# One block for each attention's layer norm and projections, by chunks of four tiles, with its elementwise work spread over three engines

## What is computed

```python
x = x + _L0_attn_ref(_layernorm(x), Wq, Wk, Wv, Wo)            # first attention, no biases
x = x + _L1_attn_ref(_layernorm(x), Wq, bq, Wk, bk, Wv, bv, ...)   # second, biased; its result is
                                                               # added to the normalised x
_layernorm(x) = (x - mean(x)) / sqrt(var(x) + eps)
q, k, v = xn @ Wq.T (+ bq), xn @ Wk.T (+ bk), xn @ Wv.T (+ bv)
```

## Time and profile before

| | us |
|---|---|
| median of three runs (2930.15 to 2933.18) | 2932.02 |
| the profiled execution | 2926.32 |
| its span, first to last instruction | 2924.5 |
| n2 and p2, from 176.3 to 250.3 of the span | 74.0 |
| n5 and p5, from 1109.5 to 1178.4 | 68.9 |

### The profile page before, as it was taken

One profiled execution on the slowest core, in us unless ns is written; L12 is line 12 of the kernel. 1 busy time (PEld: TensorE's weight loads), 2 busy tenths in 40 slices (PEclk: granted clock), 3 DMA queues, 4 the chain that ended last, 5 costly groups with the idle time before them and its releaser, 6 DMA issues. The chain is left out here.

```text
span 2924.5 us, 60113 instructions
## 1 busy us (share of the span) xinstructions
PE 2454.6 (84%) x18614; PEld 1007.0 (34%) x18614; DVE 2460.5 (84%) x3972; ACT 2229.3 (76%) x2441; POOL 1969.5 (67%) x1247
## 2 busy tenths in 40 slices
PE   2756999998586995799999999999999999983898
PEld 2642333333484663122222222222222222222566
DVE  4667888885577666899999999999999999996765
ACT  4433777777364553599999999999999999993554
POOL 4520222222463662599999999999999999994465
PEclk9966999999596997699999999999999999997799
DMA  3223100000121002100000000000000000000000
GB/s 116 70 59 98 30 28 29 28 28 12 42 60 29 1 0 71 38 16 17 15 14 14 16 16 14 14 15 16 14 14 15 16 14 14 15 5 0 1 12 18
DMA packets 93505, 76.58 MB, mean 26 GB/s; under 512 B 32481, under 2 KB 73961, under 8 KB 93265
## 3 DMA queue, kind: packets, MB, share of 16 engines
q1 hardware_dynamic: 89104, 66.36, 7.9%
q0 software_dynamic: 4288, 8.82, 0.9%
HBM read 47.77 MB, written 24.42 MB: 25 GB/s over the span
## 5 line engine op out<-in xcount | busy, mean ns | idle before, releaser
L1800 POOL TENSOR_TENSOR a_sg<-a_sg,all_f0w 128x1568 f32<-128x1568 f32 x256 | 904.9, 3535 | 21.4
L1943 ACT ACTIVATE a_pt<-a_pb 128x1024 f32<-128x1024 f32 x512 | 708.4, 1384 | 10.3 <-PE a_pb L1850 10.3
L2029 DVE TENSOR_SCALAR a_sg<-a_pa 128x1024 int32<-128x1024 int32 x512 | 615.5, 1202 | 8.0 <-PE a_pa L1850 7.9
L2018 DVE TENSOR_REDUCE a_mx<-a_pm 128x1 f32<-128x1024 f32 x507 | 613.7, 1210 | 8.8 <-PE a_pm L1850 7.3
L1952 ACT ACTIVATE a_sg<-a_sg,a_parh 128x2048 f32<-128x2048 f32 x256 | 605.1, 2364 | 15.3 <-POOL a_sg L1800 15.3
L1868 PE MATMUL a_po<-a_pt,a_Vh 128*32 128x512 f32 x2048 | 538.4, 604 | 65.0 <-ACT a_osb L1962 62.7
L1956 ACT ACTIVATE a_sg<-a_sg 128x2048 f32<-128x2048 f32 x256 | 584.1, 2282 | 0.1
L1868 PE MATMUL a_po<-a_sg,a_Vh 128*32 128x512 f32 x2048 | 538.3, 604 | 0.0
L1797 POOL TENSOR_SCALAR all_f0w<-a_sg,a_parh 128x1568 f32<-128x1568 f32 x256 | 513.9, 2007 | 27.8 <-DVE a_sg L2029 25.0
L1610 ACT ACTIVATE a_pt<-a_ring 128x1024 f32<-128x1024 f32 (+2 forms) x384 | 313.7, 846 | 150.8 <-PE a_ring L1537 147.5
L1682 DVE TENSOR_REDUCE a_mx<-a_ring 128x2 f32<-128x1024 f32 (+3 forms) x384 | 359.0, 955 | 71.6 <-PE a_ring L1520 52.6
(11 more groups left out here) (268 smaller groups left out, 4535.6 us busy)
## 6 DMA issues: line engine op xcount, KB each, us to landing
all_Q<-q_parts SPq DMA_DIRECT2D x256, 48.0 KB
all_K<-k_parts SPq DMA_DIRECT2D x256, 48.0 KB
k_parts<-p_parts SPq DMA_DIRECT2D x16, 384.0 KB, 3.1
e_recs<-routed_rows SPq DMA_DIRECT2D x70, 64.5 KB, 1.9
n_xn<-expert_rows SPq DMA_DIRECT2D x16, 256.0 KB, 4.4
all_Q<-a_rows SPq DMA_DIRECT2D x256, 2.0 KB
q_parts<-p_parts SPq DMA_DIRECT2D x16, 192.0 KB, 2.4
q_parts<-p_parts SPq DMA_DIRECT2D x8, 384.0 KB, 2.6
```

The costliest lines, as they stand in the source:

```text
L1800: nc.gpsimd.tensor_tensor(buf[:, :, 0:CUT], buf[:, :, 0:CUT], sums, ALU.mult)\
L1943: nc.scalar.activation(pt[(j - LT) % 4][:, i, :], pb[:], ACT.Exp, scale=SC)\
L2018: nc.vector.tensor_reduce(mx[:, (j // PER) % 2, t:t + 1], top[:], AX.X, ALU.max)\
L2029: nc.vector.tensor_scalar(sg[(j - ls) % 4][:, i, :].bitcast(I32), pa[:].bitcast(I32), SIGN_OFF, None, ALU.bitwise_and).then_inc(abs_done, 1)
```

## The change

The two blocks become one, `norm_project`, which goes by chunks of four tiles in 11 steps. In step k, VectorE finishes the scale of chunk k and takes the statistics of chunk k+1; ScalarE normalises chunk k (no longer VectorE), copies the transposes of chunk k-1 and splits the two pieces of chunk k-2; TensorE projects chunk k-2 and transposes chunk k-1; VectorE makes the remainders and copies the values of chunk k-2. GpSimd makes the low parts (no longer VectorE) and, in the second attention, the residual addition, one instruction for four tiles in place of four. `xn` becomes a ring of three chunks, and the transposes' PSUM ring two banks in place of four. The four chained instructions of the scale become three and a fourth that makes the bias of the normalisation. The result of the feed-forward is loaded into `XNT` in place of `xn`. The first stacks' transfers go behind pieces 6 to 11, two each, in place of three each behind pieces 8 to 11.

```diff
--- before.py
+++ after.py
...
-def ln_transposed(nc, tag, X, XNT, ident, add_to_x=False, split=None, router=None, incoming=None):
+def ln_transposed(nc, tag, X, XNT, ident, split=None, router=None, incoming=None):
...
-                def add(k):
-                    pool.wait_ge(xn_ready, k + 1)
-                    nc.gpsimd.tensor_tensor(X[:, k, :], X[:, k, :], xn[:, k, :], ALU.add).then_inc(x_added, 1)
...
-                if add_to_x:
-                    for k in range(NT):
-                        add(k)
...
-def project(nc, tag, XNT, V, qd, kd, w, weights_in, biased, ones, paired=False, constants=None, stack_loads=(),
-            cleared=None, sharpness=None):
+def norm_project(nc, tag, X, XNT, V, qd, kd, ident, w, weights_in, biased, ones, cleared, stack_loads, paired=False,
+                 incoming=None, constants=None, sharpness=None, add_to_x=False):
...
+    XR = 3
...
+        xn = m.sb("xn", [P, XR, 4, D])
         parts = m.sb("parts", [P, 4, SPLIT, CH], BF16)
         rest = m.sb("rest", [P, 4, CH])
...
+        pt = m.ps("pt", [P, 2, CH])
         psq = m.ps("psq", [P, 4, CH])
         psv = m.ps("psv", [P, 2, 4, D])
...
-        early = {i: stack_loads[n:n + 3] for n, i in zip(range(0, len(stack_loads), 3), range(8, 12))}
-
+        EARLY = 6
+        early = {i: stack_loads[n:n + 2] for n, i in zip(range(0, len(stack_loads), 2), range(EARLY, 2 * NCH))}
         pieces = range(2 * NCH)
+        steps = range(-1, NCH + 2)
...
+                if incoming is not None:
+                    for c in range(NCH):
+                        sp.dma_start(XNT[:, c * CH:(c + 1) * CH].rearrange("p (k d) -> p k d", d=D),
+                                     incoming[c * CH:(c + 1) * CH, :].rearrange("(k p) d -> p k d", p=P))\
+                            .then_inc(came[c], 16)
...
-                    if i == 8:
+                    if i == EARLY:
...
+                def low(i):
+                    pool.wait_ge(mid_done, i + 1)
+                    nc.gpsimd.tensor_tensor(parts[:, i % 4, 2, :], rest[:, i % 4, :], parts[:, i % 4, 1, :],
+                                            ALU.subtract).then_inc(lo_done, 1)
+
+                def add(c):
+                    pool.wait_ge(xn_ready, 4 * c + 4)
+                    nc.gpsimd.tensor_tensor(X[:, tiles(c), :], X[:, tiles(c), :], xn[:, c % XR], ALU.add)\
+                        .then_inc(x_added, 1)
+
+                for k in steps:
+                    if add_to_x and 0 <= k < NCH:
+                        add(k)
+                    if 0 <= k - 2:
+                        low(2 * (k - 2))
+                        low(2 * (k - 2) + 1)
+
+                def project(c, n):
+                    i = 2 * c + n
+                    if n == 0:
+                        pe.wait_ge(evacuated, c + 1)
+                    if i >= 4:
+                        pe.wait_ge(rest_done, i - 3)
+                    tokens, out = XNT[:, c * CH:(c + 1) * CH], psq[:, i % 4, :]
+                    if paired and n == 0:
+                        tokens = tokens.rearrange("p (c g n) -> p g c n", g=2, n=P)
+                        out = out.rearrange("p (g c n) -> p g c n", g=2, n=P)
+                    nc.tensor.matmul(out, (wqT, wkT)[n][:], tokens, start=True, stop=True).then_inc(q_done, 1)
+
+                def turn(c):
+                    pe.wait_ge(xn_ready, 4 * c + 4)
+                    if c >= 2:
+                        pe.wait_ge(evacuated, c - 1)
+                    for q in range(4):
+                        last = nc.tensor.transpose(pt[:, c % 2, q * P:(q + 1) * P], xn[:, c % XR, q, :], ident[:])
+                    last.then_inc(turned, 1)
+
...
+                pe.wait_ge(weights_in, loads)
+                for k in steps:
+                    if 0 <= k - 2:
+                        project(k - 2, 0)
+                        project(k - 2, 1)
+                    if 0 <= k - 1 < NCH:
+                        turn(k - 1)
+                    if 0 <= k - 2:
+                        values(k - 2)
+
+                nc.scalar.preload_act_table_set("natural_log_exp_and_others")
...
+                def root(c):
+                    act.wait_ge(ve_ready, c + 1)
+                    nc.scalar.activation(rs[:, tiles(c)], ve[:, tiles(c)], ACT.Ln).then_inc(ln_var, 1)
+                    act.wait_ge(ln_var, c + 1)
+                    nc.scalar.activation(rs[:, tiles(c)], rs[:, tiles(c)], ACT.Exp, scale=-0.5).then_inc(rs_ready, 1)
+
+                def normalise(c):
+                    act.wait_ge(scaled, c + 1)
+                    if c >= XR:
+                        act.wait_ge(turned, c - XR + 1)
+                        if add_to_x:
+                            act.wait_ge(x_added, c - XR + 1)
+                    for q in range(4):
+                        k = 4 * c + q
+                        nc.scalar.activation(xn[:, c % XR, q, :], X[:, k, :], ACT.Identity, bias=offset[:, k:k + 1],
+                                             scale=rstd[:, k:k + 1]).then_inc(xn_ready, 1)
+
+                def evacuate(c):
+                    act.wait_ge(turned, c + 1)
+                    nc.scalar.activation(XNT[:, c * CH:(c + 1) * CH], pt[:, c % 2, :], ACT.Copy).then_inc(evacuated, 1)
...
-                high(0)
-                for i in pieces[1:]:
-                    high(i)
-                    middle(i - 1)
-                middle(pieces[-1])
+                for k in steps:
+                    if 0 <= k - 2:
+                        high(2 * (k - 2))
+                    if 0 <= k < NCH:
+                        normalise(k)
+                    if 0 <= k - 2:
+                        high(2 * (k - 2) + 1)
+                    if 0 <= k - 1 < NCH:
+                        evacuate(k - 1)
+                    if 0 <= k - 2:
+                        middle(2 * (k - 2))
+                        middle(2 * (k - 2) + 1)
+                    if k + 1 < NCH:
+                        root(k + 1)
+                nc.vector.memset(V[:, :, :, DH:DH + 1], ones).then_inc(ones_set, 1)
...
+                def statistics(c):
+                    if incoming is not None:
+                        dve.wait_ge(came[c], 16)
+                        nc.vector.tensor_tensor(X[:, tiles(c), :], X[:, tiles(c), :],
+                                                XNT[:, c * CH:(c + 1) * CH].rearrange("p (k d) -> p k d", d=D), ALU.add)\
+                            .then_inc(summed, 1)
+                        dve.wait_ge(summed, c + 1)
+                    for k in range(4 * c, 4 * c + 4):
+                        nc.vector.bn_stats(stats[:, k, :], X[:, k, :]).then_inc(stats_done, 1)
+                    for k in range(4 * c, 4 * c + 4):
+                        dve.wait_ge(stats_done, k + 1)
+                        nc.vector.bn_aggr(mv[:, k, :], stats[:, k, :]).then_inc(mv_done, 1)
+                    dve.wait_ge(mv_done, 4 * c + 4)
+                    nc.vector.tensor_scalar(ve[:, tiles(c)], mv[:, tiles(c), 1], LN_EPS, None, ALU.add)\
+                        .then_inc(ve_ready, 1)
+
+                def scale(c):
+                    t = tiles(c)
+                    dve.wait_ge(ve_ready, c + 1)
+                    dve.wait_ge(rs_ready, c + 1)
+                    link = Chain(dve, newton, 3 * c)
+                    link(nc.vector.tensor_tensor(t1[:, t], rs[:, t], rs[:, t], ALU.mult))
+                    link(nc.vector.scalar_tensor_tensor(t1[:, t], t1[:, t], -0.5, ve[:, t], ALU.mult, ALU.mult))
+                    link(nc.vector.scalar_tensor_tensor(rstd[:, t], t1[:, t], 1.5, rs[:, t], ALU.add, ALU.mult))
+                    nc.vector.scalar_tensor_tensor(offset[:, t], mv[:, t, 0], -1.0, rstd[:, t], ALU.mult, ALU.mult)\
+                        .then_inc(scaled, 1)
...
-                def low(i):
-                    dve.wait_ge(mid_done, i + 1)
-                    nc.vector.tensor_tensor(parts[:, i % 4, 2, :], rest[:, i % 4, :], parts[:, i % 4, 1, :],
-                                            ALU.subtract).then_inc(lo_done, 1)
...
-                for c in range(NCH):
-                    rest_of(2 * c)
-                    if c:
-                        low(2 * c - 1)
-                    rest_of(2 * c + 1)
-                    if c:
-                        values(c - 1)
-                    low(2 * c)
-                low(2 * NCH - 1)
-                values(NCH - 1)
+                for k in steps:
+                    if 0 <= k < NCH:
+                        scale(k)
+                    if k + 1 < NCH:
+                        statistics(k + 1)
+                    if 0 <= k - 2:
+                        rest_of(2 * (k - 2))
+                        rest_of(2 * (k - 2) + 1)
+                        values(k - 2)
...
-            lambda: ln_transposed(nc, "n2", X, XNT, ident, incoming=y_d),
...
-            lambda: ln_transposed(nc, "n5", X, XNT, ident, add_to_x=True),
```

(36 more changed lines are left out.)

11 lines of the change are left out of this document (10 added, 1 removed).

## The result

The changed kernel takes 2908.56 us (median of four runs, 2905.2 to 2914.46), the kernel before on the same chip 2931.09 (2929.64 to 2933.18): a ratio of 0.9926, 95% interval 0.991 to 0.9941. The forecast was 2908.0.

What follows compares the result with a forecast made beforehand. No engine bounds the two stretches; two loops run one after the other. Steps of 6.4 and 6.2 us save 12.1 and 11.9, together 24.0, so 2932.0 - 24.0 = 2908 us; range for 8 in 10: 2896 to 2922.

Steps and rivals of the forecast that it cites:

- The bound: In both old stretches, 142.9 us in all, no engine bounds; two loops run in turn, each bound by what the other leaves free.
- The collision: VectorE's scale links with two SBUF inputs wait for GpSimd's running low part: 1.1 us a step, bounds 0 and 2.3.
- The step: New block's period per chunk: 6.4 us in the first attention, 6.2 in the second; without collision 5.3 and 5.0.
- the drain: Block's end: step 7 without root, last steps, way to next block: 5.9, 7.0, 3.8 us first attention; 5.7, 7.1, 3.9 second.
- root 7: Moment when ScalarE's root for chunk 7's scale is ready: 221.5 in the first attention, 1149.8 in the second.
- A slot of the ring is needed again two steps later: Store ring of pieces: a slot is needed again two steps (12.6 us) after its `high`, so SyncE keeps up.
- The clock: TensorE's level in the new block, 1.2 or 2.4 GHz, costs little: a chunk takes 6.4 us low, some 3.3 high.
- its floor: Where the collision is absent, TensorE's low clock puts a floor of 6.4 us under the step.
- At the engines' pace: Rival, chance 0.22: no collision and the high clock, steps of 5.3 and 5.0 us, 11.5 more saved, 2896.5.
- The upper bound of the collision: Rival, chance 0.2: two blocked links of 1.16 us each, or low clock in series; steps of 7.6, 2921.
- Slower by the store ring: Rival, chance 0.04: ScalarE waits for store slots, normalisation with it; decides from 17.4 us per piece, `high` to landing.
- The attentions as long as before: Sign of being right: the attentions behind the two changed stretches keep their length.

Runs made afterwards that it cites:

- low_between: Changed kernel, but GpSimd's first low part of a step waits for the scale or incoming sum, the second until `ve` is made: 2904.06 us, 0.9906 of before.
- changed_again: The changed kernel run once more, unaltered, as a control: 2908.98 us, 0.9925 of the kernel before.
- ring6_alone: Changed kernel with the ring of parts and stores six pieces long instead of four, low parts left as they were: 2905.90 us, 0.9913 of before.
- low_between_ring6: `low_between` with six slots instead of four in the ring of parts and stores: 2898.90 us, 0.988 of before; repeated 2900.79 us, 0.9891.
- low_on_vector: Changed kernel, but VectorE makes the low parts again, after the values of the same step: 2908.70 us, 0.9912 of before.
- low_after_scale: Changed kernel, but GpSimd starts a step's two low parts only after VectorE's incoming sum (first attention) or the scale's input reads (second): 2903.97 us, 0.9901 of before.

## Why the prediction was right

**The bound, right.** Two loops, each bound by what the other left free; laid side by side they gave 21.2 us. Each half gives its own part.

**The collision, right, with its size.** I took one blocked link of 1.1 a step. Measured: 0.22 to 0.31 and 1.07 to 1.09 in the links, 0.16 each without it, together 1.0. `low_between` shows its price by taking it away: 6.02 to 5.06. What I did not see is that it reaches instructions with one input: `ve` is held up as well where a low part runs beside it. The trace of before has such a row in n5, beside GpSimd's additions:

```profile
1127.13 3.06 DVE L157 TENSOR_SCALAR n_xn<-all_X,n_mv,n_rstd 128x128 f32<-128x128 f32 x8
```

The same eight tiles take 2.14 in n2, where GpSimd is idle. In the changed kernel no low part runs beside a `ve`; one `ve` of the second attention met an addition and took 0.26 us, 0.41 in `changed_again`.

**The step, right in kind, 0.2 to 0.4 too long.** Forecast 6.4 and 6.2, measured 6.02 and 6.01. Without the collision 5.06 and 4.96, for 5.3 and 5.0: VectorE's way was 0.2 too long in my sum, ScalarE's right. Steps of 6.0 lie below the 6.2 to 6.4 that I named as the sign.

**The term that failed: the drain.** I let it run at the engines' pace, 16.7 us from root 7 to the next block in both attentions. Measured: 19.5 (218.43 to 237.89) and 19.6 (1135.42 to 1155.04), from the first link behind root 7; 19.4 and 19.1 in `changed_again`. In the first, `high` waited 3.0 us for stores (forecast: no DMA among its waits); in the second 1.3, and 1.5 more for the last matmuls (0.84 and 0.70). "A slot of the ring is needed again two steps later" holds for full steps only; from step 8 to step 9 `high` comes 3.35 us later (224.08, 227.43). The last pieces and their waits (ScalarE, profile after):

```profile
227.43 0.60 ACT L1186 ACTIVATE p_parts<-p_psq 128x512 bf16<-128x512 f32 x1 [0.37 <-DMA q_parts<-p_parts]
230.62 0.60 ACT L1186 ACTIVATE p_parts<-p_psq 128x512 bf16<-128x512 f32 x1 [2.60 <-DMA k_parts<-p_parts]
```

The waits for stores are not the whole of it. `ring6_alone` has none, and its drains still take 18.5 and 18.8. So of the 2.8 and 2.9 us too little the store waits account for 0.9 and 0.8: without them `high` waits for the last matmuls, 2.4 and 1.9 us in all. In the first attention the first of them took 2.07 us, the level of 1.2 GHz:

```profile
225.10 0.60 ACT L1187 ACTIVATE p_parts<-p_psq 128x512 bf16<-128x512 f32 x1 [1.12 <-PE p_psq L1129]
226.51 0.60 ACT L1187 ACTIVATE p_parts<-p_psq 128x512 bf16<-128x512 f32 x1 [0.81 <-PE p_psq L1129]
```

Where both are absent, in the first attention of `low_between_ring6`, the engines needed 12.1 us from the first link behind root 7 to the last low part (215.11 to 227.20), for the 12.8 of my sum, and the way of the last stores made 18.8 of it. So the engines' part was priced right. What I had at nothing was the ring of stores and the last matmuls' low clock, and what I had too short was the way of the last stores; one or another of them held the drain in each of these three kernels.

In the first attention root 7 came 2.5 us sooner than forecast and the drain took 2.8 longer, which cancels: 61.9 forecast, 62.2 measured. In the second root 7 came only 0.4 sooner, and the stretch is 59.5 for 57.0. Of the forecast 24.0 us 21.2 came in the stretches; the medians' 22.5 holds another 1.3 within the scatter of the unchanged part. That the forecast met the median within 1 us is partly this luck: by the stretches alone it was 2.8 too low.

**The clock, right that it costs little, its floor unproved.** Two steps of the first attention, TensorE:

```profile
210.82 1.13 PE L1128 MATMUL p_psq<-all_XNT,all_wqT 128*128 128x512 f32 x2 [2.70 <-ACT all_XNT L1180]
...
216.84 2.08 PE L1128 MATMUL p_psq<-all_XNT,all_wqT 128*128 128x512 f32 x2 [2.70 <-ACT all_XNT L1180]
```

The first ran at 2.4 GHz and the second at 1.2 (granted clock 1.00 from 210.82, 0.50 from 216.84), and both steps take 6.0. The whole chunk at the low level took 6.1 us, from 216.84 to the next piece at 222.97, so 6.4 was a little high; its 1.5 for the second piece came from a matmul of 1.64 us, where one wholly at the low level takes 1.92 (at 218.71). The floor under a step without the collision was not tested: in the first attention's full steps of `low_between_ring6` the pieces took 1.12 and 1.02 us, the high level, and the steps were 5.03 to 5.05.

**Engine choice.** The Trainium skill, "GPSIMD Engine Reference", section "Engine selection", speaks for VectorE in elementwise work. A low part took 1.155 us on GpSimd (0.679 before), but what that cost was not the duration: `low_on_vector` and the changed kernel take the same time, and with its instructions placed GpSimd is 5.0 us ahead in the stretches (115.5 against 120.5, `low_between` and `low_on_vector`); their medians are 4.6 apart, with ratios whose intervals overlap.

**The rivals.** "At the engines' pace" was priced at 2896.5; taking away the collision and, in the drain, the store waits gave 2898.9 and 2900.8. The upper bound of the collision did not come: only one low part a step meets the second link, and the third starts when GpSimd is done. Its price was also 1.5 us too high: in the second attention two blocked links make 5.0 + 2.3 = 7.3 of a step, not 7.6. "Slower by the store ring" needed 17.4 us from `high` to landing in the full steps, and there `high` never waited for a store; in the drain it waited 3.0 and 1.3 us. No table load lay inside a block. "The attentions as long as before" holds by the last column of the table (2789.1 and 2786.9), not by the one pair of profiles.

The best version here is `low_between_ring6`: 0.988 and 0.9891 of the kernel before, and in its stretches 7.7 to 8.8 us shorter than the changed kernel.

## What to carry to other kernels

Where GpSimd is given work, ask not only how long it takes but what VectorE does in that time: a short link of a dependent chain (0.16 us) may take as long as GpSimd's instruction (1.1), and waits that put GpSimd beside statistics, or beside reads of PSUM, get it back. After a ring has been taken off the path in the steady steps, look at its drain, where slots are needed again sooner, and price the last stores themselves as well. And do not let an early instruction of a new order wait for the first matmuls at the low clock with the critical one behind it.

## What the runs showed of the hardware

- A one-input `TENSOR_SCALAR` of 128 x 4 took 1.16 us beside a GpSimd low part and 0.17 elsewhere, while `BATCH_NORM_STATS2` (0.87 for four tiles) and `BATCH_NORM_AGGREGATE` (0.36) beside the low part ahead of it kept their time (`low_after_scale`). The Trainium skill, "SBUF — State Buffer", section "SBUF: two separate sides", names VectorE's two-port modes beside instructions with two SBUF inputs as users of the shared ports. That agrees, if this instruction runs in such a mode; no run shows its mode.
- Between two GpSimd instructions in a row VectorE got its turn: the first link ended with the first low part (200.38 + 0.22 = 200.60; 199.43 + 1.155 = 200.59), and only then did the second low part hold up the second link. Where the first link came just behind the first low part's end, in the second attention, it took 1.11 us, ended with the second (1111.48 + 1.11 = 1112.59; 1110.30 + 2.27 = 1112.57), and the second link took 0.16. So no link here waited for two.
- TensorE at 210.82 and at 216.84 had stood still the same 2.70 us and got different clocks, 2.4 and 1.2 GHz; in the second attention likewise, 1.2 at 1127.99 behind 2.70 us and 2.4 at 1140.02 behind 2.71.
